# Unread TensorE products ahead of the first scores of the third and fifth attention block

## What is computed

```python
Xn = (X - mu) * rsqrt(var + EPS) * ln_g + ln_b
Q, K, V = split_heads(Xn @ Wq + bq), split_heads(Xn @ Wk + bk), split_heads(Xn @ Wv + bv)
scores = einsum('bhqd,bhkd->bhqk', Q, K) / sqrt(16)          # causal: masked with -inf above the diagonal
x = layernorm(X + einsum('bhqk,bhkd->bhqd', softmax(scores), V) @ Wo + bo)
h = relu(x @ W1 + b1)
alpha = softmax(h @ W2 + b2)                                 # 8 weights for each row
out = layernorm(x + sum_k alpha_k * (U_k @ (V_k @ x)))
```

## Time and profile before

| what | us |
|---|---|
| median of 3 runs | 457.18 |
| lowest and highest | 456.28, 459.7 |
| the profiled execution, its own time | 456.41 |
| its span, first to last instruction | 454.5 |

### The profile page before, as it was taken

One profiled execution on the slowest core, in us unless ns is written; L12 is line 12 of the kernel. 1 busy time (PEld: TensorE's weight loads), 2 busy tenths in 40 slices (PEclk: granted clock), 3 DMA queues, 4 the chain that ended last, 5 costly groups with the idle time before them and its releaser, 6 DMA issues.

```text
span 454.5 us, 7238 instructions
## 1 busy us (share of the span) xinstructions
PE 414.0 (91%) x2541; PEld 207.3 (46%) x2541; DVE 313.7 (69%) x805; ACT 234.0 (51%) x498; POOL 73.2 (16%) x108
## 2 busy tenths in 40 slices
PE   7988896998999989999999997999899998998892
PEld 3445442343344433376557733334334343346562
DVE  5538994798798783337478898579889782125476
ACT  7661554665767575443441353566666857522210
POOL 2331220143120010101130022013212010010000
PEclk9999996999999999999999999699999999999997
DMA  6066660360402000001663135045030000000011
GB/s 186 5 99 99 172 105 15 48 92 5 72 2 94 3 1 0 1 1 62 121 115 52 49 52 90 1 64 79 11 62 3 0 3 0 2 0 0 1 47 46
DMA packets 18435, 21.13 MB, mean 46 GB/s; under 512 B 4960, under 2 KB 11872, under 8 KB 18400
## 3 DMA queue, kind: packets, MB, share of 16 engines
q1 hardware_dynamic: 18349, 20.66, 24.2%
q10 hardware_dynamic: 51, 0.01, 0.0%
HBM read 5.79 MB, written 2.10 MB: 17 GB/s over the span
## 4 chain that ended last, share of the span: by engine, by line
PE 67%; DVE 16%; ACT 7%; SPq 4%; DMA 3%; issue 3%; POOL 1%; DVEq 0%; ACTq 0%
PE ps L775 25%; PE ps L877 13%; PE ps L857 13%; PE ps L836 10%; DVE mx L661 9%; PE ps L840 2%; ACT pr L559 2%; DMA stq<-mrow 2%; SPq L448 2%; ACT stk L517 2%; SPq L449 2%; PE ps L766 1%; PE ps L922 1%; PE ps L887 1%; DVE x L619 1%
## 5 line engine op out<-in xcount | busy, mean ns | idle before, releaser
L559 ACT ACTIVATE pr<-ps 128x512 f32<-128x512 f32 (+3 forms) x384 | 167.1, 496 | 112.1 <-PE ps L857 110.5
L661 DVE TENSOR_REDUCE mx<-ps 128x1 f32<-128x512 f32 (+3 forms) x304 | 182.1, 654 | 35.1 <-PE ps L840 26.5
L857 PE MATMUL ps<-stq,stk 99*128 99x512 bf16 (+3 forms) x384 | 118.8, 337 | 14.3 <-DMA stq<-mrow 9.0
L836 PE MATMUL ps<-stk,stq 96*128 96x512 bf16 (+3 forms) x384 | 115.4, 332 | 2.4 <-DVE mx L661 1.3
L507 POOL TENSOR_SCALAR_AFFINE_SELECT pr<-pr 128x512 f32<-128x512 f32 x64 | 40.6, 635 | 261.0 <-ACT pr L559 261.0
L877 PE MATMUL ps<-pr,va 128*32 128x512 f32 (+3 forms) x768 | 82.3, 501 | 0.0
L857 PEld LDWEIGHTS ps<-stq,stk 99*128 99x128 bf16 x384 | 35.0, 99 | 102.0 <-ACT pr L559 51.5
L840 PE MATMUL ps<-mask,ident_b 128*128 128x128 bf16 x256 | 50.2, 222 | 0.0
L836 PEld LDWEIGHTS ps<-stk,stq 96*128 96x128 bf16 x384 | 37.9, 99 | 20.4 <-issue 6.9
L840 PEld LDWEIGHTS ps<-mask,ident_b 128*128 128x128 bf16 x256 | 25.7, 100 | 13.3 <-issue 4.4
L775 PE MATMUL ps<-u_t,avt 128*128 128x256 f32 x128 | 30.6, 383 | 0.0
(11 more groups left out here) (80 smaller groups left out, 356.2 us busy)
## 6 DMA issues: line engine op xcount, KB each, us to landing
stq<-qk_raw SPq DMA_DIRECT2D x32, 96.0 KB, 2.8
stk<-qk_raw SPq DMA_DIRECT2D x32, 96.0 KB, 2.8
x_in<-in_x SPq DMA_DIRECT2D x8, 256.0 KB, 4.4
stq<-qk_raw SPq DMA_DIRECT2D x32, 64.0 KB, 2.4
stk<-qk_raw SPq DMA_DIRECT2D x32, 64.0 KB, 2.4
out_y<-x SPq DMA_DIRECT2D x3, 512.0 KB, 3.0
stk<-qk_raw SPq DMA_DIRECT2D x32, 32.0 KB, 2.4
stq<-qk_raw SPq DMA_DIRECT2D x32, 32.0 KB, 2.1
```

The lines of the kernel that those rows point to most:

```text
L559: nc.scalar.activation(probs(b, g, s)[:, j, q0 - c * CHUNK:], act_bank(ev)[:, q0 - c * CHUNK:], ACT.Exp, scale=DH ** -0.5).then_inc(s_act_ ...
L661: nc.vector.tensor_reduce(dst, src, AX.X, ALU.max).then_inc(s_dve_free, 1)
L836: last = nc.tensor.matmul(bank[:, i * w:(i + 1) * w], q[0:ROWS, t // TPC, j, tile(t % TPC)], k[0:ROWS, k0 // CHUNK, j, 0:w], start=True, s ...
L857: nc.tensor.matmul(bank[:, q0 - c * CHUNK:], stk[stack_of(b, g)][0:ROWS + PARTS, kt // TPC, j, tile(kt % TPC)], stq[stack_of(b, g)][0:ROWS ...
```

## The change

`turn_over` gets the bank as an argument. The two calls at the start keep `values_bank` and their counts. A third call is new: in the chunk c = 1, ahead of the first score of group 0 (the third block) 13 products are made, and ahead of that of group 1 (the fifth block) six, in both sequences. They go into the very bank that the score then overwrites, so `take_act` is moved ahead of them and of the wait for the rows. In all 38 products are added (2 x 13 + 2 x 6), each with its own load of the stationary operand.

```diff
-            def turn_over(n):
+            def turn_over(bank, n):
                 for _ in range(n):
-                    nc.tensor.matmul(values_bank, ident_b[:], ident_b[:].unsqueeze(1).to_broadcast([P, TPC, P]),
+                    nc.tensor.matmul(bank, ident_b[:], ident_b[:].unsqueeze(1).to_broadcast([P, TPC, P]),
                                      start=True, stop=True)
...
-            turn_over(20)
+            turn_over(values_bank, 20)
...
                     if ev == ("xt", 0, 0, KC - 1):
-                        turn_over(5)
+                        turn_over(values_bank, 5)
...
                 if kind == "score":
                     _, _, g, s, j = ev
                     c, kt, q0, _ = steps[s]
+                    bank = take_act(ev)
                     if kt == 0 and j == 0:
+                        if c and g < 2:
+                            turn_over(bank, 6 if g else 13)
                         if b == g == c == 0:
                             pe.wait_ge(s_minus, STACKS)
                         pe.wait_ge(s_rows[c], 16 * (b * G + g + 1))
-                    bank = take_act(ev)
```

## The result

| | before | after |
|---|---|---|
| median of 4 runs, us | 458.44 (456.28 to 460.11) | 451.59 (450.77 to 453.09) |
| profiled execution, us | 456.41 | 450.77 |
| its span, us | 454.5 | 449.0 |
| mean granted clock of its span | 0.978 | 0.994 |

The ratio is 0.9879, with a 95% interval of 0.9843 to 0.9914. A second set on another occasion, 6 runs beside 11 of the kernel before, gave 451.95 against 457.14 us, ratio 0.9884 (0.9852 to 0.9915). So the change saves 1.2%, some 5.5 us. The plain difference of the medians is 6.85 us in the first set, of four scattered runs each, and 5.19 us in the second. The forecast was 452.1 us, 5.05 us less than before.

What follows compares the result with a forecast made beforehand. TensorE, busy 91% of the span, was taken as the bound, slowed by half clock behind the third blocks' waits. 2.01 + 3.05 less 0.01 makes 5.05 us; 457.18 - 5.05 = 452.1 us, range 450.9 to 455.3.

Steps and rivals of the forecast that it cites:

- The base of the forecast: Median of the kernel before, 457.18 us, from which 5.05 us were taken to give 452.1 us.
- What is given back: Full clock in the third blocks' first two steps returns 2.01 us in the first sequence, 3.05 us in the second.
- The first steps: Third block's first step, 3.69 us in both sequences, falls to 1.99 us at full clock, giving 1.70 us each.
- the way between the first scores: From the third to the fifth block's first score, both sequences take about 31.9 us without the fold.
- The cost of the products: The 38 products, 0.215 us apart, hide in the waits ahead of the third and fifth blocks; cost 0.01 us.
- That the clock is the cause: Behind the third blocks' waits TensorE works 4.35 and 6.51 us at 1.2 GHz instead of 2.4.
- The idle rest in the first sequence: Ahead of the third block, 0.97 us stay idle between the 13 products' end and the rows' arrival.
- the bound of 0.29 us on the product spacing: Above this spacing, 13 products would hold TensorE past the rows' arrival at the first sequence's third block.
- The rival of half the gain: Clock still falls ahead of one third block, or a later wait takes the gain: 454.1 or 455.2 us; chance 0.10.
- The rival with an overhang: Products hold TensorE past the rows' arrival at all four places, 7.05 us in sum: 464.2 us; chance 0.07.
- Other executions: The change should act on other executions as on the profiled one, which was 0.77 us faster than the median.

Runs made afterwards that it cites:

- plus_seven: The changed kernel with seven unread products more at each of the four places (20 and 13 instead of 13 and six): 457.42 us, ratio 0.9991.
- fifth_only: The changed kernel with the fifth block's six products alone, none ahead of the third block: 457.03 us, ratio 0.9993 to the kernel before.

## Why the prediction was right

- **The time as a whole.** 452.1 us were forecast and 451.59 measured, and this closeness is partly luck. The base of the forecast, 457.18 us, became 458.44 with a fourth run; from there 5.05 us less is 453.4. The terms below don't depend on that base.
- **What is given back.** 5.06 us were forecast, 2.01 + 3.05 by sequence; the ledger has 1.96 + 2.99 = 4.95. The first steps were to take 1.99 us and take 2.03, the way between the first scores was to be about 31.9 us without the fold, and is 32.91 - 1.01 = 31.90 and 31.94.
- **The cost of the products.** 13 x 0.215 = 2.80 us were forecast, 2.86 and 2.82 stand there. In the first row of the ledger there is no loss, nor at the fifth blocks (rows issued at 102.29 in the changed kernel, score 2.37 us later, as before). The rival with an overhang was priced rightly per product, by `plus_seven`, but didn't occur.
- **That the clock is the cause.** Three ways lead to it: with no products at the third block the clock falls and nothing is gained, with three it falls and nothing measurable is gained, and among runs of one kernel the time goes with the mean clock at about half a microsecond for each microsecond at half.
- **The idle rest in the first sequence.** Forecast 0.9 us, found none in this execution and 0.80 in the next. The forecast took SP's late issue for fixed. It is one long DMA issue, there in 12 of 14 profiled executions, and the bound of 0.29 us on the product spacing holds only when it comes.
- **The rival of half the gain.** Its reason, an idle rest behind the products with thin work ahead, was real but too weak at 0.8 us: with six products even 2.01 us passed in one execution. The rule of the Trainium skill that spoke for it ("TensorE: Matmul & The Clock Gate", Part 2, "Back-to-back issue gap", 131 ns per pair in a stream) doesn't hold for these products: 0.22 us each here, with a weight load each.
- **Other executions.** The profiled execution of before was taken to stand for the others. It did in that all 57 further runs of the kernel before have a mean clock of 0.985 or less, and all ten of the changed kernel 0.990 or more. How often and how long the clock falls varies from run to run all the same, as the prediction had allowed: 0.972 to 0.985 before, and 6 of the 10 runs of the changed kernel show no further fall by their mean clock, the rest one short one. That makes most of its spread of 450.8 to 453.6 us; the six at 0.994 alone spread from 450.77 to 452.0.

## What to carry to other kernels

Read the granted clock behind every longer wait of TensorE, in more than one execution: what such a wait costs may lie behind it, in steps that look merely slow. At the third blocks the clock fell behind 1.95 us and more in every trace but one (2.01 us) and not at 1.41 us, but this is no bound for other places: it fell once behind 1.19 us and passed once behind 2.44 us. A wait that can't be removed can be filled with products that nobody reads, counted so that they end just before what is waited for; one too many costs its full length. Better is real work moved into the wait, if something else fills the rest; recount the unread products of later waits afterwards, since these may be gone.

## What was not expected of the hardware

- The clock fell behind an idle stretch of 1.95 us and not behind one of 2.01 us with three more products ahead of it. Behind the same wait of 1.92 or 1.93 us near 420 us it fell in four profiled executions and not in eight.
- At the third block of the first sequence it was low for 6.8 us in the profiled execution of before, behind a wait of 3.70 us, and for 3.4 us in that of `fifth_only`, behind 2.82 us. The second sequence of `fifth_only` had 6.8 us behind 2.78 us, so the length of the wait doesn't set that of the fall.
- Single SP issues of stack DMAs take up to 1.96 us instead of 0.59, at changing places in each of the 14 profiled executions. One of them moves the first sequence's rows by up to 1 us.
- Short stretches of 3.4 us at half clock came up at places that the first profile didn't show: near 15, 47 and 422 us, behind waits of TensorE of 2.86, 1.19 or 1.30, and 1.92 us. Whether the six products of the fifth block prevent such a one stays open.
